# The opening of a perceiver layer on one Trainium2 core, reordered by key chunks, with filler matmuls for TensorE

## The reference, cut to what matters

```python
def _L0_xattn_ref(latents, context, ...):
    lat = layernorm(latents, ln_l_w, ln_l_b)          # 128 rows x 256
    ctx = layernorm(context, ln_c_w, ln_c_b)          # 12544 rows x 256
    q = (lat @ Wq) ...                                # 16 heads of 64
    k, v = split(ctx @ Wkv)
    attn = softmax(clip(q @ k.T * 64**-0.5, -11, 11))
    return (attn @ v) @ Wo + bo
x = x + _L0_xattn_ref(layernorm(x), ctx_1024, ...)
x = x + _L0_attn_ref(layernorm(x), ...)               # self attention over the 128 rows, with LoRA
x = x + _L0_ffn_ref(layernorm(x), ...)                # fp8 linear
```

## Time and profile before

| | us |
|---|---|
| median of 3 runs (1159.00, 1160.93, 1162.26) | 1160.93 |
| time of the profiled execution | 1157.79 |
| its span | 1156.1 |
| PE busy in it | 1137.3 (98%) |
| DVE, ACT, POOL busy | 829.5, 598.8, 309.0 |

### The profile page before, as it was taken

The page is one execution under the profiler, slowest core; times in us unless marked ns, Lnnn a source line. Parts: engine busy times, 40 slices in busy tenths (PEclk is TensorE's granted clock), DMA queues, the critical chain, the costliest instruction groups (busy, mean ns, idle before and its releaser), DMA issues.

```text
span 1156.1 us, 18331 instructions
## 1 busy us (share of the span) xinstructions
PE 1137.3 (98%) x5056; PEld 936.4 (81%) x5056; DVE 829.5 (72%) x1622; ACT 598.8 (52%) x1029; POOL 309.0 (27%) x516
## 2 busy tenths in 40 slices
PE   6999999999999999999999999999999999999997
PEld 5888888888888888888888888888888888888774
DVE  5778778777777777787776776776766766766624
ACT  4555555555555555555555555555555555555411
POOL 5334334334334233242221221221211211211100
PEclk8999999999999999999999999999999999999996
DMA  5221221221211211354212212212112112110000
GB/s 178 69 69 46 68 68 45 68 63 51 68 61 53 68 55 59 108 108 81 74 46 69 67 46 68 62 51 68 57 56 68 53 61 68 51 64 24 1 1 5
DMA packets 81393, 70.72 MB, mean 61 GB/s; under 512 B 40115, under 2 KB 67670, under 8 KB 81366
## 3 DMA queue, kind: packets, MB, share of 16 engines
q1 hardware_dynamic: 80390, 68.94, 20.1%
q10 hardware_dynamic: 976, 1.45, 0.4%
HBM read 70.13 MB, written 0.13 MB: 61 GB/s over the span
## 4 chain that ended last, share of the span: by engine, by line
PE 96%; issue 2%; DMA 1%; DVE 1%; POOL 0%; ACT 0%; SPq 0%; POOLq 0%; DVEq 0%; ACTq 0%
PE bank L466 31%; PE bank L467 31%; PE bank L468 31%; PE bank L511 1%; DMA wkT<-in_WkT_dram 1%; PE bank L572 1%; PE bank L584 1%; PE bank L503 0%; PE bank L614 0%; PE bank L596 0%; PE bank L630 0%; PE bank L594 0%; POOL wkT L457 0%; DVE fold_y L909 0%; PE bank L604 0%
## 5 line engine op out<-in xcount | busy, mean ns | idle before, releaser
L732 ACT ACTIVATE ex<-bank,c_rstd 128x512 f32<-128x512 f32 x392 | 270.1, 689 | 242.4 <-PE bank L468 166.4
L403 POOL TENSOR_TENSOR z_lo<-z,z_hi 128x255 fp32r<-128x255 f32 x196 | 174.9, 892 | 742.1 <-ACT z_hi L745 742.1
L739 ACT CAST p_hi<-ex 128x512 fp32r<-128x512 f32 x392 | 243.8, 622 | 240.8 <-DVE ex L899 148.6
L903 DVE TENSOR_TENSOR p_lo<-ex,p_hi 128x512 fp32r<-128x512 f32 x392 | 271.6, 693 | 116.3 <-ACT p_hi L739 99.7
L466 PE MATMUL bank<-qk_hi,d_hi 128*128 128x512 f32 x784 | 305.9, 390 | 0.0
L467 PE MATMUL bank<-qk_lo,d_hi 128*128 128x512 f32 x784 | 305.5, 390 | 0.0
L466 PE MATMUL bank<-p_hi,z_hi 128*128 128x512 f32 x784 | 305.5, 390 | 0.0
L468 PE MATMUL bank<-p_hi,z_lo 128*128 128x512 f32 x784 | 305.5, 390 | 0.0
L468 PE MATMUL bank<-qk_hi,d_lo 128*128 128x512 f32 x784 | 305.3, 389 | 0.0
L467 PE MATMUL bank<-p_lo,z_hi 128*128 128x512 f32 x784 | 305.2, 389 | 0.0
L899 DVE TENSOR_SCALAR ex<-ex 128x512 f32<-128x512 f32 x392 | 189.8, 484 | 156.5 <-ACT ex L732 154.6
(11 more groups left out here) (162 smaller groups left out, 410.0 us busy)
## 6 DMA issues: line engine op xcount, KB each, us to landing
t_all<-in_ctxT_dram SPq DMA_DIRECT2D x98, 384.0 KB, 3.2
x_pair<-in_ctx_dram SPq DMA_DIRECT2D x98, 256.0 KB, 2.7
diff<-sig_all SPq DMA_DIRECT2D x194, 0.5 KB, 1.9
wq<-in_Wq_dram ACTq DMA_DIRECT2D x2, 512.0 KB, 6.9
wkT<-in_WkT_dram SPq DMA_DIRECT2D x2, 512.0 KB, 6.1
wv<-in_Wv_dram SPq DMA_DIRECT2D x1, 1024.0 KB
wo<-in_Wo_dram SPq DMA_DIRECT2D x1, 1024.0 KB
crow_all<-in_crows_dram ACTq DMA_DIRECT2D x1, 256.0 KB, 7.6
```

The costliest lines, as they stand in the source:

```text
L403: pool.tensor_tensor(z_lo[s][:, b, 0:LAST], z[s][:, b, 0:LAST], z_hi[s][:, b, 0:LAST].bitcast(F32), ALU.subtract).then_inc(s_zlo, 1)
L732: act.activation(ex[c][:, :], sc_bank[c][:, :], ACT.Exp, scale=c_rstd[s4][:, b:b + 1])\
L739: act.copy(p_hi[b][c][:, :], ex[c][:, :]).then_inc(s_phi, 1)
L903: dve.tensor_tensor(p_lo[b][c][:, :], ex[c][:, :], p_hi[b][c][:, :].bitcast(F32), ALU.subtract)\
```

## The change

The opening is rearranged; the loop's steps and the work after the loop stay as they are.

- Loads: x, pair 0 rows, Wq half 0, pair 0 transposed, Wq half 1, pairs 1, 2, WkT half 1, pair 3 on SP, with no wait between them; small columns, the two rows as one row of one partition (`crow_one`), and WkT half 0 on ACT. The host lays out context and Wq so that each partition reads one contiguous piece.
- The two layer norm rows are spread over the partitions by a matmul of height 1 (L535) and copied from PSUM by ACT.
- PE starts with 22 matmuls on zeros (`keep_warm_r`) and, behind the spreading one, 3 on `ident` (`keep_warm`). Their results are used by nobody.
- The chunks of `qk` are formed from other blocks: chunk c takes both head halves of blocks m = 2c, 2c+1. So chunk 0 needs only folds and centres 0 and 1, and queries 0 and 1. `qk_block` alternates between the two 64-row halves. DVE, ACT and PE do chunk 0 first, and folds and centres 2 and 3 behind it.
- `q_heads(1)` moves between the first scores of chunk 0 and those of chunk 1. PE then waits for its scaled copy (`s_qT`) ahead of the first loop pair.
- The statistics of pair 1 move on DVE behind the first clip, `difference(1)` and `difference(2)` move from POOL to DVE.

```diff
+            def keep_warm_r():
+                still, cols = z_lo[0][:, 0, 0:P], z_lo[0][:, 1, 0:P]
+                halves = [slice(0, P // 2), slice(P // 2, P)]
+                for _ in range(6):
+                    pe.matmul(bank[5][:, 0:P], still, cols, start=True, stop=True)
+                for n in range(12):
+                    pe.matmul(bank[n % 2][:, 0:P], still[halves[n % 2], :], cols[halves[n % 2], :], start=True, stop=True)
+                for n in range(4):
+                    pe.matmul(bank[2][:, 0:2 * P], still, z_lo[0][:, 1, :], start=True, stop=True)
+            pe.wait_ge(s_zero, 1)
+            keep_warm_r()
             pe.wait_ge(s_const, 1)
+            pe.wait_ge(s_const, 2)
+            pe.wait_ge(s_crows, 16)
+            pe.matmul(bank[4][:, 0:2 * D], ones_row[:, :], crow_one[:, :], start=True, stop=True).then_inc(s_crowp, 1)
+            keep_warm(3)
...
+            for c in range(CH):
+                pe.wait_ge(s_qT, c + 1)
+                pe.wait_ge(s_wkE, CM * (c + 1))
+                pe.wait_ge(s_fold, 2 * CM * (c + 1))
                 for k in range(KD):
-                    qk_block(0, k, a, bank[2 * k + a])
-            q_heads(1, bank[6])
+                    if (c, k) == (1, 1):
+                        pe.wait_ge(s_qklo, 1)
+                    qk_block(0, k, CHUNK_M[c], [QK_WIDE[c][k][:, a, :] for a in range(2)])
             pe.wait_ge(s_row0, 1)
             for c in range(CH):
                 pe.wait_ge(s_qklo, KD * (c + 1))
                 scores(0, 0, 0, 0, c, first=True)
+                if c == 0:
+                    pe.wait_ge(s_wq[1], 16)
+                    q_heads(1, range(MH), bank[3])
+            pe.wait_ge(s_qT, CH + 1)
...
 # DVE
+            dve.wait_ge(s_wkT[0], 16)
+            dve.wait_ge(s_crow, 1)
+            fold(0)
+            fold(1)
             first_stats(0)
...
+            tile_z(0, 0, 0, 0, used=False)
+            clip(0, 0)
+            tile_z(0, 0, 0, 1, used=False)
             first_stats(1)
```

More of the change, by code:

```diff
@@ L29, in perceiver_layer @@
     _, N, D = x.shape
-    S = ctx.shape[1]
-    INNER = Wq.shape[1]
+    PAIRS, INNER = ctx.shape[0], WkT.shape[1] * P
+    S = PAIRS * 2 * P
     H = 16
@@ L45, in perceiver_layer @@
     MH = MI // PASSES
+    CM = MH // CH
     SLOTS = 4
@@ L274, in perceiver_layer @@
         QK_PAIRS = (45, 46)
+        Q_BANK = (bank[7], bank[5])
+        QK_WIDE = ((wide[0], wide[1]), (wide[3], wide[0]))
+        CHUNK_M = [range(c * CM, (c + 1) * CM) for c in range(CH)]
         def passes(eng, pair):
@@ L496, in weighted_sum, with q_heads @@
                 ins.then_inc(s_pv, 1)
-            def q_heads(half, dst):
-                pe.wait_ge(s_wq[half], 16)
-                for m in range(half * MH, (half + 1) * MH):
+            def q_heads(half, ms, dst):
+                for m in ms:
                     for k in range(KD):
-                        ins = pe.matmul(dst[:, (m % MH) * P:(m % MH + 1) * P], wq[:, k, m * P:(m + 1) * P],
-                                        latT[:, k, :], start=(k == 0), stop=(k == KD - 1))
+                        ins = pe.matmul(dst[:, m * P:(m + 1) * P], wq[:, half, k, m * P:(m + 1) * P], latT[:, k, :],
+                                        start=(k == 0), stop=(k == KD - 1))
@@ L505, in q_heads, with qk_block @@
                 ins.then_inc(s_qTp, 1)
[L507 to L513, removed]
+            def qk_block(half, k, ms, dsts):
+                for m in ms:
+                    for a in range(2):
+                        hd = slice(a * DH, (a + 1) * DH)
+                        ins = pe.matmul(dsts[a][:, m * P:(m + 1) * P], wkE[hd, half * MH + m, k * P:(k + 1) * P],
+                                        qT[hd, half * MH + m, :], start=True, stop=True)
+                        if m == ms[-1]:
+                            ins.then_inc(s_qkp, 1)
@@ new lines, in keep_warm @@
+            def keep_warm(n):
+                for _ in range(n):
+                    pe.matmul(bank[5][:, 0:P], ident[:, :], ident[:, :], start=True, stop=True)
+            def keep_warm_r():
[7 more added lines that the diff above has]
+                    pe.matmul(bank[2][:, 0:2 * P], still, z_lo[0][:, 1, :], start=True, stop=True)
@@ L558, in pair @@
                         pe.wait_ge(s_qklo, KD * CH + CH * k)
-                    for a in range(CH):
-                        qk_block(1, k, a, bank[6 + a])
+                    qk_block(1, k, range(MH), (bank[6], bank[7]))
             passes(pe, pair)
@@ L752, in _ @@
                                scale=lat_w[:, k:k + 1]).then_inc(s_latT, 1)
-            for m in range(MH):
-                centre(m)
-            qT_scaled(0, bank[7])
+            centre(0)
+            centre(1)
+            for c in range(CH):
+                qT_scaled(c, 0, CHUNK_M[c], Q_BANK[c])
             act.wait_ge(s_sigp, 1)
```

164 lines of the change are left out of this document (83 added, 81 removed).

## The result

| | before | changed |
|---|---|---|
| median of 12 runs, us | 1160.33 | 1164.64 |
| lowest to highest | 1156.10 to 1163.39 | 1163.80 to 1166.40 |
| profiled execution: time, span | 1157.79, 1156.1 | 1163.80, 1162.0 |
| first scores start | 24.02 | 18.66 |
| first weighted sum (the mark) | 28.46 | 32.11 |

A forecast was written before the change was run, and what follows sets the result against it. PE, busy from 24.0 to 1093.5 us, bounds the kernel, so only the loop's start moves: 0.9 + 2.0 = +2.9 on 1157.8 is 1160.7; that execution lies 3.1 below the median, so 1164, range 1158 to 1169.

The forecast's parts named there:

- The first scores near 17.5: Opening on PE: the first scores would start at 17.5 us instead of 24.02, 6.5 us earlier.
- PE waits 1.8 us for centres 2 and 3: Opening: PE would wait 1.8 us ahead of the products of chunk 1, for centres 2 and 3 from ACT.
- The products at 1.7 us: Opening and loop (pair 45): 16 half-height product instructions would keep their 1.7 us despite alternating halves.
- my rival: Half-height matmuls run side by side: 0.8 us less at each loop place and in chunk 1, about 1161.6; chance 0.12.
- The chain to the sigma row of pair 1: Opening, first exponential to `qT`: late statistics, POOL, SP, DMA and `d_hi` would run from 18.9 to 28.0 us.
- PE stands for 6 us: Ahead of the second scores: PE would stand still for 6 us, from 22.1, waiting for ACT's `qT`.
- The clock: Behind the stall: the clock would fall, 4 us at the lower level costing +2.0 us, between 0 and 3.5.
- The rival of a low clock in the first chunk: Opening: clock stays low through first chunk, slowing products, first scores and part of queries; +4.0, about 1168; chance 0.25.
- The mark at +0.9: First weighted sum: it would start at 29.4 us instead of 28.46, +0.9 us, before the charge for the clock.
- The filler: Start of PE: as a rival, filler gives full clock from about 5 us; -1.7, about 1159.2; chance 0.18.

The follow-up runs named there:

- the one move: The changed kernel with ACT's scaling of the half 1 queries (`qT`) moved ahead of `d_hi(1)`: 1160.11 us, ratio to before 1.0002.
- the other: The changed kernel with the statistics and difference of pair 1 moved forward on DVE, behind fold 3: 1159.43 us, ratio to before 1.0003.

## Why the prediction was right, step by step

- **Direction and size.** Forecast 1164.0, measured 1164.64. On the profiled execution I had +2.9 up to the loop's end and found +3.4. That is closer than the terms deserve, and in that part luck: the late start (+1.4) and the clock (+0.2) are for the most part cancelled by the products (-1.1). The medians differ by 4.3, and the 0.9 beyond the 3.4 is not accounted for. I gave slower by over 0.3% a chance of 0.40 and no change 0.48; the result lies just over that line.
- **The first scores near 17.5.** 18.66. Two terms were mis-sized. The filler ended at 5.5 (5.0), the spreading at 7.5 (6.7) and the second filler at 9.1 (8.1), so the queries started at 10.62, not 9.5. I took 0.16 us for one of their instructions, between 0.107 and 0.22, and they took 3.50/16 = 0.22, the lower level's duration. So they ended at 14.1 and not 12.1. The foldings were late too: WkT landed at 8.2, where I had it by 7.4. The products, 0.55 us shorter in each chunk, took back 1.1 of the delay.
- **PE waits 1.8 us for centres 2 and 3.** 1.82.
- **The products at 1.7 us.** Wrong: 1.16 in the opening and in the loop. I kept the row's duration because its weight loads were filled. The gain is 0.55 us per 16 and not the 0.8 of my rival, which was right as a mechanism, and came on top of the forecast. The Trainium skill, page "TensorEngine Tiling (Array Packing)", section "Key Properties", says that different tiles can load weights and multiply in parallel; the trace agrees in kind.
- **The chain to the sigma row of pair 1.** From the first exponential to the end of `qT` I had 18.9 to 28.0, 9.1 us; the trace has 20.41 to 29.33, 8.9. The link that I named (late statistics, POOL, SP, DMA, `d_hi`, `qT`) is the one in the rows; the one move removes the stall of 5.90 us, the other 3.0 us of it.
- **PE stands for 6 us.** 5.90. The start and the end of the wait are both 1.4 us later than forecast.
- **The clock.** I charged 2.0 us, 4 us of work at the lower level; it was 4.8 us of work and cost 2.2. The rival of a low clock in the first chunk didn't occur in the profiled execution of the changed kernel, where the products and first scores ran at the higher level, but it did in two experiments' (the early statistics, and six matmuls in the stall). In the second of them the edit stands behind that point, so there it is a matter of the execution.
- **The mark at +0.9, with the clock behind it apart.** The late start behind the stall is +2.3, of which 1.4 is the late opening; clock +2.2; the products of the loop -1.1, which I had at nothing.
- **The filler.** I asked only whether it would raise the clock early. It didn't: without it the queries take 3.78 us instead of 3.50. Its cost, 1 to 1.5 us, lay in my sum as the delay of `latT`.

What stays open: which part of the rearrangement (the order of the loads, the layout on the host, the spreading by a matmul, the chunks) wins the 5.4 us at the first scores, since no run takes them apart; what decides in which executions the clock falls in the products of chunk 1 and where it falls behind the loop.

## What to carry to other kernels

When work is pulled forward to start a pipeline earlier, follow every operand of the second stage as well: here 5.4 us were won at the first scores, and 9 us of chain that the old slow opening had hidden (statistics, four small POOL steps, a DMA, an in-order list on ACT) took them all and more. An engine's list is in order, so a cheap instruction that everyone needs must not stand behind one that waits for a DMA; look for it at the first idle row behind the point that was won. Work that filled the idle engine kept its clock up and still won nothing that the medians show, since the true operands were as late as before, and filler ahead of a first operand can only be judged by what the operand's own start loses.

## What the runs showed of the hardware

- Float32 matmuls of 64 rows that alternate between the two halves of the array took 1.16 us for 16 instructions, 0.07 each, against 1.71, 0.107 each, with four matmuls of one half in a row. The columns, the banks and the clock were the same. With two matmuls of one half in a row it was 1.23 to 1.26.
- The windows print a granted clock of 1.00 for the first 14 us of the changed kernel and of the one without filler, in which full-height float32 instructions of 128 columns took 0.22 to 0.24 us, twice the 0.12 (1.95/16) of the same instruction at 20.15. The duration of a known instruction is the better reading there.
- A small step on POOL took some 0.4 us longer where it began 0.17 to 0.27 us behind the start of a DVE tensor_tensor of 128x512. In the changed kernel the first step took 1.08 and 1.06 us for pairs 0 and 1 (DVE was in `diff` and in `p_lo`) and 0.70 for the third pair, with DVE idle. Before, the second step took 1.02 and 1.11 (DVE in `diff` and in `d_lo`), with no idle time of POOL ahead of it. The copy of 0.18 us took 0.71 and 0.72 where it began just behind `p_lo`. These are coincidences in time in several traces; no run moved one of the two alone.
- One kernel's executions differ by 2.6 to 8 us, along with their mean granted clock (for the kernel with early statistics, 1162.7 us at 0.984 and 1157.6 at 0.989). A comparison of two profiled executions must say at what clock they ran.
